# A 6-layer windowed-attention network on one core: the centred input moved to another PSUM bank, and the network's steps moved within a hand-written order

## The reference, cut to what matters

```python
x = attn_layer(shift_tokens(x), Wqkv[i], q_scale[i], k_scale[i], Wo[i]) + x
x = ffn_layer(shift_tokens(x), ln_g[i], ln_b[i], W1[i], b1[i], W2[i], b2[i]) + x

# attn_layer: 16 heads of 64, windows of 32 tokens, each looks at itself and the one before
q = l2norm(q) * qs; k = l2norm(k) * ksc            # then rotary tables with a scale
sim = q k^T * 8 (masked); out = softmax(sim) @ v; return out @ Wo
# ffn_layer, hidden size 341
xn = (x - mean) / sqrt(var + 1e-5) * g + bln
a, gate = split(xn @ W1 + b1); return (a * gelu(gate)) @ W2 + b2
```

## Time and profile before

| what | value |
|---|---|
| median of 3 runs | 3764.9 us (3754.34 to 3772.09) |
| the profiled execution's own time | 3773.0 us, of it span 3771.0 us |
| busy share of the span: PE, DVE, POOL, ACT | 90%, 87%, 75%, 65% |
| mean granted TensorE clock | 0.962 of full speed |
| waits, total: POOL `sin_part` for DVE `normed` | 622.0 us |
| waits, total: ACT `to_raw` for DVE `rotated` | 483.8 us |
| waits, total: PE `norm_back_ffn` for ACT `ffn_normed` | 76.7 us |

### The profile page before, as it was taken

One profiled execution on the slowest core, in us unless ns is written; L12 is line 12 of the kernel. 1 busy time (PEld: TensorE's weight loads), 2 busy tenths in 40 slices (PEclk: granted clock), 3 DMA queues, 4 the chain that ended last, 5 costly groups with the idle time before them and its releaser, 6 DMA issues.

```text
span 3771.0 us, 107872 instructions
## 1 busy us (share of the span) xinstructions
PE 3375.2 (90%) x45916; PEld 2204.0 (58%) x46108; DVE 3287.8 (87%) x2914; ACT 2435.9 (65%) x3945; POOL 2810.7 (75%) x1265
## 2 busy tenths in 40 slices
PE   5758999998999999999998999899999999999987
PEld 3325665665665665665666666565666656666664
DVE  6758999998999988999898998898988988998992
ACT  4645766766766766666666676666666666666764
POOL 4457788778787778778777778877777887887771
PEclk9879999999999999999999999999999999999996
DMA  2001111121111111111111111121111111111111
GB/s 72 1 1 36 36 34 38 34 58 41 35 34 39 34 51 44 39 34 35 36 52 44 33 35 35 31 50 44 39 33 34 38 46 45 39 37 35 34 37 36
DMA packets 129694, 141.98 MB, mean 38 GB/s; under 512 B 35388, under 2 KB 73152, under 8 KB 129216
## 3 DMA queue, kind: packets, MB, share of 16 engines
q1 hardware_dynamic: 129216, 135.09, 14.5%
HBM read 19.62 MB, written 2.10 MB: 6 GB/s over the span
## 4 chain that ended last, share of the span: by engine, by line
PE 33%; DVE 23%; POOL 18%; issue 12%; ACT 4%; SPq 3%; DMA 2%; POOLq 0%; ACTq 0%; DVEq 0%
PE bank L570 10%; POOL rr L1138 8%; POOL swp L1148 5%; PE mid L620 4%; DVE Pr L1362 4%; DVE rot L1398 4%; PE mid L579 4%; DVE raw L1390 4%; PE bank L639 4%; PE bank L668 3%; DVE rot L1404 3%; PE mid L607 2%; PE mid L627 2%; DVE ss L1384 2%; PE bank L676 2%
## 5 line engine op out<-in xcount | busy, mean ns | idle before, releaser
L1148 POOL TENSOR_TENSOR swp<-raw,TS 128x1024 f32<-128x1024 f32 x384 | 899.6, 2370 | 622.0 <-DVE raw L1390 622.0
L570 PE MATMUL bank<-wqkv,xs 128*128 128x512 f32 x2304 | 1206.9, 627 | 24.1 <-DMA xs<-F 8.6
L1138 POOL TENSOR_TENSOR rr<-ssm,nhalf 128x32 f32<-128x32 f32 x192 | 1214.8, 6327 | 16.0
L896 ACT ACTIVATE raw<-bank 128x512 f32<-128x512 f32 x768 | 434.6, 592 | 545.0 <-DVE rot L1404 483.8
L579 PEld LDWEIGHTS mid<-ident,rot 128*128 128x128 f32 x3072 | 367.8, 143 | 387.7 <-issue 335.9
L579 PE MATMUL mid<-ident,rot 128*128 128x128 f32 x3072 | 444.6, 278 | 132.7 <-DVE rot L1404 127.3
L1384 DVE TENSOR_REDUCE ss<-sq 128x16 f32<-128x1024 f32 x384 | 463.6, 1207 | 112.1 <-ACT sq L904 111.3
L570 PEld LDWEIGHTS bank<-wqkv,xs 128*128 128x128 f32 x2304 | 387.3, 193 | 289.9 <-issue 194.0
L1390 DVE TENSOR_TENSOR raw<-raw,rr 128x2048 f32<-128x2048 f32 x192 | 469.3, 2444 | 42.6 <-POOL rr L1138 42.6
L1398 DVE TENSOR_TENSOR rot<-raw,TC 128x2048 f32<-128x2048 f32 x192 | 442.2, 2303 | 52.6 <-PE mid L579 51.1
L1404 DVE TENSOR_TENSOR rot<-rot,swp 128x2048 f32<-128x2048 f32 x192 | 440.2, 2292 | 21.0 <-DVE rot L1398 1.4
(11 more groups left out here) (132 smaller groups left out, 4340.8 us busy)
## 6 DMA issues: line engine op xcount, KB each, us to landing
PT<-PTd SPq DMA_DIRECT2D x1344, 64.0 KB
xs<-F SPq DMA_DIRECT2D x192, 64.0 KB, 1.9
BT<-PTd SPq DMA_DIRECT2D x192, 64.0 KB
wqkv<-d_wqkv SPq DMA_DIRECT2D x36, 256.0 KB, 2.8
fwo<-d_fwo SPq DMA_DIRECT2D x6, 512.0 KB, 4.3
d_out<-X SPq DMA_DIRECT2D x8, 256.0 KB, 2.3
w<-d_w SPq DMA_DIRECT2D x6, 341.0 KB
w<-d_w SPq DMA_DIRECT2D x6, 128.0 KB
```

The lines of the kernel that those rows point to most:

```text
L570: nc.tensor.matmul(bank[bk][:, :], xs[:, j, :], wqkv[:, c, :], start=True, stop=True)\
L1138: pool.tensor_tensor(rr[:, :], ssm[:, :], nhalf[:, :], ALU.pow).then_inc(rr_ready, 1)
L1148: last = pool.tensor_tensor(dst[:, :, :, t, :], src[:, :, :, 1 - t, :], tab.unsqueeze(2).broadcast_to([P, 2, HEADS, 32]), ALU.mult)
```

## The change

Five edits, all in the order or in the choice of a bank:

1. `centred` writes bank 7 in place of bank 6. `ffn_stats` and `ffn_normed` read it there, `centred` waits until bank 7 is out (`yo_ready` of the batch before), and `out_proj` of a batch's first tile waits for `xo_ready` in place of `xn_ready`.
2. PE: `qk_back` 2 and 3 go from behind `proj` 1 of a slot to the end of the slot before. `proj` 0 goes ahead of `qk_back` 0. `norm_back_ffn` goes from ahead of `proj` 5 to behind `out_proj`; `ffn_in(1,0)` to the end of slot 0; `ffn_in(2,0)` from behind `proj` 4 to ahead of `pv`; `ffn_out` from behind `proj` 3 to ahead of it.
3. ACT: `to_raw` 1 waits for `sin_part` and `cos_part` of the tile two before, in place of its `rotated`. `to_raw` 0 goes ahead of `qk_to_sbuf` 0 and `to_raw` 2 ahead of `squares` 0. `ffn_normed` goes behind `squares` 1, `ffn_affine` ahead of `to_v` 4, `gelu` 1 from behind `qk_to_sbuf` 3 to ahead of `to_v` 5, `lin_to_sbuf` 0 from behind to ahead of `to_raw` 3, `lin_to_sbuf` 2 from behind `to_v` 4 to ahead of `squares` 0, `ffn_to_sbuf` from the end of slot 2 to behind the first `to_raw` of slot 3, `attn_to_sbuf` ahead of `to_v` 4.
4. POOL: `gated` 0 and `gated` 2 go ahead of `sin_part` in slot 1.
5. DVE: `ffn_stats` goes ahead of `rotated`.

The core of the diff (the PE list of `c % 4 == 2` as it becomes, and the edits on the other engines; the other PE lists change as said above):

```diff
@@ out_proj, centred (PE)
                 if j == 0:
-                    wait(pe, xn_ready, b)
+                    wait(pe, xo_ready, b)
...
-                    mm = nc.tensor.matmul(bank[6][:, t * P:(t + 1) * P], FX[:, t * P:(t + 1) * P], cen[:, :],
+                    mm = nc.tensor.matmul(bank[7][:, t * P:(t + 1) * P], FX[:, t * P:(t + 1) * P], cen[:, :],
@@ slot (PE), c % TPB == 2, the waits on banks left out
                     step(c, 0, proj, 1, True, 0)
-                    step(c, 3, qk_back, 2, False)
-                    step(c, 3, qk_back, 3, False)
                     batch(c, 2, ffn_in, 1, 1, False, 7)
                     step(c, 0, proj, 3, False, 1)
                     batch(c, 2, ffn_in, 2, 1, False, 7)
                     step(c, 3, scores)
                     batch(c, 2, ffn_in, 0, 0, False, 7)
+                    step(c, 0, proj, 0, False, 0)
                     step(c, 2, qk_back, 0, True)
-                    step(c, 0, proj, 0, False, 0)
                     step(c, 0, proj, 2, False, 1)
+                    batch(c, 2, ffn_in, 2, 0, False, 7)
                     step(c, 4, pv)
                     step(c, 3, proj, 4, False, 0)
-                    batch(c, 2, ffn_in, 2, 0, False, 7)
                     step(c, 3, proj, 5, False, 1)
                     step(c, 2, qk_back, 1, False)
                     step(c, 4, out_proj)
+                    step(c, 2, qk_back, 2, False)
+                    step(c, 2, qk_back, 3, False)
@@ to_raw (ACT)
-                    wait(act, rot_ready, n - 1)
+                    wait(act, sin_ready, n - 1)
+                    wait(act, cos_ready, n - 1)
@@ slot (ACT), c % TPB == 1
                     step(c, 3, to_v, 4)
                     batch(c, 2, gelu, 0)
+                    batch(c, 2, gelu, 1)
                     step(c, 3, to_v, 5)
                     step(c, 2, qk_to_sbuf, 2)
                     step(c, 2, qk_to_sbuf, 3)
-                    batch(c, 2, gelu, 1)
                     batch(c, 2, gelu, 2)
@@ slot (ACT), c % TPB == 2
                     step(c, 0, to_raw, 1, True)
+                    batch(c, 2, lin_to_sbuf, 0)
                     step(c, 0, to_raw, 3, False)
-                    batch(c, 2, lin_to_sbuf, 0)
+                    step(c, 0, to_raw, 0, False)
                     step(c, 2, qk_to_sbuf, 0)
-                    step(c, 0, to_raw, 0, False)
+                    step(c, 0, to_raw, 2, False)
+                    batch(c, 2, lin_to_sbuf, 2)
                     step(c, 0, squares, 0)
-                    step(c, 0, to_raw, 2, False)
                     step(c, 3, exps)
                     step(c, 4, o_to_sbuf)
                     step(c, 0, squares, 1)
                     step(c, 2, qk_to_sbuf, 1)
                     step(c, 3, to_v, 4)
-                    batch(c, 2, lin_to_sbuf, 2)
                     step(c, 3, to_v, 5)
                     step(c, 2, qk_to_sbuf, 2)
                     step(c, 2, qk_to_sbuf, 3)
-                    batch(c, 2, ffn_to_sbuf)
@@ slot (POOL), c % TPB == 1
                     batch(c, 2, gated, 1)
+                    batch(c, 2, gated, 0)
+                    batch(c, 2, gated, 2)
                     step(c, 0, sin_part)
-                    batch(c, 2, gated, 0)
                 elif c % TPB == 2:
-                    batch(c, 2, gated, 2)
@@ slot (DVE), c % TPB == 3
                     step(c, 1, cos_part)
+                    batch(c, 1, ffn_stats)
                     step(c, 1, rotated)
-                    batch(c, 1, ffn_stats)
```

More of the change, by code:

```diff
@@ L697, in slot @@
[L697 to L728, removed]
@@ L740, in slot @@
                     step(c, 4, out_proj)
-                elif c % TPB == 2:
+                    after_batch(c, (2, xn_ready), (3, yo_ready), (3, lin_out[2]), (3, lin_out[0]), (3, ge_ready[2]), (3, ge_ready[1]), (3, ge_ready[0]), (3, lin_out[1]), (3, nT_out))
+                    batch(c, 2, norm_back_ffn)
+                    after(c, (4, oT_out), (2, qkT_out[0]), (3, qkT_out[2]))
+                    step(c, 2, qk_back, 2, False)
+                    after(c, (2, qkT_out[1]), (4, oT_out), (3, qkT_out[3]))
@@ L742, in slot @@
+                    step(c, 2, qk_back, 3, False)
+                    after_batch(c, (2, nT_out), (2, xn_ready), (3, yo_ready), (3, lin_out[2]), (3, lin_out[0]), (3, ge_ready[2]), (3, ge_ready[1]), (3, ge_ready[0]), (3, lin_out[1]))
+                    batch(c, 2, ffn_in, 1, 0, True, 7)
+                elif c % TPB == 1:
                     after(c, (4, v_out[0]), (1, raw_out[0]), (1, raw_out[1]))
                     step(c, 0, proj, 1, True, 0)
-                    after(c, (5, oT_out), (3, qkT_out[0]), (4, qkT_out[2]))
@@ L745, in slot @@
[L745 to L749, removed]
                     after(c, (4, v_out[1]), (1, raw_out[2]), (1, raw_out[3]))
                     step(c, 0, proj, 3, False, 1)
-                    after_batch(c, (2, ge_ready[1]), (2, ge_ready[0]), (2, lin_out[1]), (2, nT_out), (3, yo_ready), (3, lin_out[2]), (3, lin_out[0]), (3, ge_ready[2]))
@@ L757, in slot @@
-                    batch(c, 2, ffn_in, 0, 0, False, 7)
+                    after(c, (0, raw_out[1]), (4, v_out[0]), (1, raw_out[0]))
+                    step(c, 0, proj, 0, False, 0)
                     after(c, (3, qkT_out[2]), (5, oT_out), (3, qkT_out[0]))
                     step(c, 2, qk_back, 0, True)
-                    after(c, (0, raw_out[1]), (4, v_out[0]), (1, raw_out[0]))
-                    step(c, 0, proj, 0, False, 0)
-                    after(c, (0, raw_out[3]), (4, v_out[1]), (1, raw_out[2]))
@@ L979, in ffn_normed @@
                 for t in range(TPB):
-                    last = nc.scalar.activation(xn[:, t, :], bank[6][:, t * P:(t + 1) * P], ACT.Copy,
+                    last = nc.scalar.activation(xn[:, t, :], bank[7][:, t * P:(t + 1) * P], ACT.Copy,
                                                 scale=rstd[:, t:t + 1])
@@ L1049, in slot @@
                     step(c, 2, qk_to_sbuf, 3)
-                    batch(c, 2, ffn_to_sbuf)
                 else:
                     step(c, 0, to_raw, 1, True)
+                    batch(c, 2, ffn_to_sbuf)
                     step(c, 0, to_raw, 3, False)
+                    step(c, 0, to_raw, 0, False)
                     step(c, 2, qk_to_sbuf, 0)
-                    step(c, 0, to_raw, 0, False)
+                    step(c, 0, to_raw, 2, False)
                     step(c, 0, squares, 0)
-                    step(c, 0, to_raw, 2, False)
                     step(c, 3, exps)
@@ L1061, in slot @@
                     step(c, 2, qk_to_sbuf, 1)
+                    batch(c, 1, attn_to_sbuf)
                     step(c, 3, to_v, 4)
-                    batch(c, 1, attn_to_sbuf)
                     step(c, 3, to_v, 5)
```

120 lines of the change are left out of this document (78 added, 42 removed).

## The result

| | before | changed |
|---|---|---|
| median of 5 runs | 3757.7 us (3747.0 to 3772.1) | 3784.2 us (3780.4 to 3789.0) |
| profiled execution | 3773.0 us, span 3771.0 | 3784.2 us, span 3782.3 |
| mean granted clock | 0.962 | 0.979 |

The ratio changed over before is 1.0067, with a 95% interval of 1.0039 to 1.0095: slightly slower, and clear of no change by the interval.

The account below looks back on a forecast made before the run. DVE and what stands around it were taken to set three of four stretches, PE the third. 69.48 + 0.1 + 2.35 - 0.2 + 0.2 = 71.9 us per batch against 71.84 gave 3768 us, range 3725 to 3805.

Parts of the forecast that it names:

- loop of 16.28 us: From DVE's transpose through SP's DMAs, pv, its copy, squares 1, sumsq and probs to the next transpose; floor of every interval.
- interval 1: First of a batch's four times between DVE's probs_back transposes, 16.28 us undisturbed; forecast +0.1, bounds 0 and +0.8.
- Interval 2: Second time between transposes, where PE is full; forecast 20.5 in place of 18.15 us, +2.35, bounds +0.9 and +2.9.
- Chain (a): In interval 2, to_v 5 waits for gelu 1 and its product, so PE's proj 3 starts 1.45 us late.
- chain (b): In interval 2, ACT's lin_to_sbuf 0 ahead of to_raw 3 waits for its product; exps ends 2.8 us later.
- rival A: Interval 2's chains are met by slack and cost about +0.9; 3697 us, or 3655 with interval 2 unchanged; chance 0.28.
- The disturbance: POOL's power under rotated makes rstd late, PE idles 3.61 us, the clock falls; forecast to go, gaining 1.2 to 2.36.
- Interval 4: Fourth time between transposes, 17.50 us undisturbed; to_v 4 delays proj 1, proj 3 and centred; +0.2, bounds 0 and +1.0.
- undisturbed batch: The one batch whose intervals of 16.28, 18.15, 17.55 and 17.50 us, together 69.48, were the base of the forecast.
- Interval 3: Third time between transposes, 17.55 us undisturbed; -0.2 as ffn_y is no longer beside normed, bounds -0.7 and +0.4.
- the 2.36: us a mean batch of 71.84 loses to what comes and goes; 0.65 of it is normed slowed by POOL's ffn_y.
- Rival B: The disturbance stays or moves and the clock still falls; 1.2 to 2 us per batch, 3825 to 3862 us; chance 0.22.

Follow-up runs that it names:

- e1_gelu: Changed kernel with gelu 1 on ACT put back behind qk_to_sbuf 3, so to_v 5 is ahead of it; 3727 us, ratio to before 0.9892.
- e4_settle: Kernel before with only bank 7, norm_back_ffn and ffn_normed later, ffn_affine ahead of to_v 4, ffn_stats ahead of rotated; 3762 us, ratio 0.9989.
- e6_fill: Kernel before with N, S and F together; 3723 us, ratio to before 0.9857.
- N: Piece: norm_back_ffn and ffn_normed later, ffn_affine ahead of to_v 4, bank 7 with its waits; alone on the kernel before, ratio 1.0001.
- S: Piece: ffn_stats ahead of rotated on DVE; not run alone.
- F: Piece: proj 0 ahead of qk_back 0, to_raw 1 waiting for sin_part and cos_part, to_raw 0 and 2 earlier; alone on the kernel before, ratio 0.9992.
- e12_vpe: e3_both with the addition of epsilon ahead of rstd moved from POOL to DVE behind ffn_stats; 3689 us, ratio to before 0.9822.
- e3_both: Changed kernel with gelu 1, lin_to_sbuf 0 and 2, ffn_in(2,0) and POOL's gated 0 and 2 in their old order; 3705 us, ratio to before 0.9839.

## Why the prediction was right

**Bounds and loop.** That DVE and the loop of 16.28 us set interval 1 and PE interval 2 held: interval 1 is 16.38 in the mean and never under 16.2, and in slot 2 of the changed kernel PE is busy for 18.81 of 19.18 us:

```profile
1687.19:1706.37 19.18, 18.81 (x248) 11.54 (x248) 16.03 (x12) 13.33 (x22) 14.58 (x7) 1.00 0.14 32
```

**Interval 2**, +2.35 forecast. `proj` 3 was to start 3.6 us after the transpose and started 3.50 after (1680.82 - 1677.32); the wait was to be 1.3 to 1.45 and is 1.27; `exps` was to end 16.1 us behind the transpose and ended 15.78 behind it (1692.04 + 1.06 - 1677.32), and the next transpose was to follow 4.4 us later and followed after 4.34. The interval was to be 20.5 and is 19.99. Chain (a) costs 1.30 us when it is undone, chain (b) with POOL's order 0.84. The prediction took `normed` of this interval at its undisturbed length, and it is 0.6 us longer; this was hidden under `exps`. The term decided the sign, and rival A, which would have had it at +0.9, is out by the 19.99 and by e1_gelu.

**The disturbance.** That it goes away was right: the clock falls 0 times where it fell 19 times, and the 76.7 us that PE waited for `xn` are 12.8. The power no longer starts under `rotated`, which it did in 15 of 44 batches, and beside `ffn_stats` it took its 5.46 us in all 22 batches in which it started there, as forecast. But my reason was incomplete. I gave it to two pieces, valued the earlier `to_raw` at nothing ("Nothing gains"), and gave `proj` 0 ahead of `qk_back` 0 no term at all. By e4_settle and e6_fill the two are worth 1.3% once N and S are in. The step that failed was to ask of F only what it does to the loop, not what PE does while it waits: with N and S alone PE stood up to 2.92 us for `rot`, and the clock fell 33 times in 44 batches.

**Interval 4**, +0.2 forecast, is 1.1 us over the undisturbed 17.50. The term is mis-sized by 0.9. Of the 1.1, 0.74 us lie between `normed` and the transpose (8.92, where the undisturbed batch has 1575.90 - 1567.72 = 8.18). I followed the power out from under `rotated`, and not what then comes behind it, `rstd`, which now begins within 0.05 us of `normed` and takes 2 us more; e12_vpe brings this part back to 8.17. The other 0.4 us lie ahead of `normed` (9.73 for 9.32), where `cos_part` lasts 2.60 us in the mean for 2.25. They are gone in e3_both (9.26), so they came with the exchanges of slots 1 and 2; their cause stays open. The prediction has the rule for such pairs, a DVE operation with two SBUF inputs and a GpSimd operation, and I used it for the power and not for `rstd`.

**Interval 3** was forecast at 17.4 (-0.2) and is 17.15. Against the mean of before, 18.05, it is 0.9 shorter, and 0.67 of that is `normed`, which `ffn_y` no longer meets. But the -0.2 was taken from the undisturbed batch, and there `normed` of this interval already lasted 2.28 us, so it had no source; the 0.4 us that came lie ahead of `normed` (9.00 for 1550.24 - 1540.85 = 9.39). And the 0.65 us per batch of long `normed`, which the prediction counted in the 2.36 and let go, are still 0.60: they stand in interval 2 now.

**The sum** was 71.9 per batch and is 72.17. The errors of -0.5, -0.25 and +0.9 nearly cancel, so that the total is closer than its terms is luck. The forecast of +3 us on the profiled execution's 3773.0 met +11; the 3768 by the median met 3784, within the range of 3725 to 3805 that the forecast had for itself. Measured from the median of before, 3757.7, the forecast of +3 us met +26.5. The upper end of that range doesn't follow from its terms: over the forecast they give 0.7 + 0.55 + 0.6 + 0.8 + 1.2 = 3.85 us, half of which is 73.8 us per batch and not 72.7. Rival B is out, since the clock never fell. By the bound of 0.5% it is slower, where I gave 0.34, less than to faster, 0.40; I had given rival A too much.
